# Graph attention: fp32 scores computed once, with targets on partitions, and turned exponentials

## What is computed

```python
q = (x @ wq + bq).reshape(n, H, C)        # H = 2, C = 64; k and v alike
alpha = einsum('ehc,ehc->eh', q[dst], k[src]) / sqrt(C)
amax  = segment_max(alpha, dst)           # 0 where a node has no edge
ex    = exp(alpha - amax[dst])
a     = ex / (segment_sum(ex, dst)[dst] + 1e-16)
out   = segment_sum(a[:, :, None] * v[src], dst).mean(axis=1) + x @ ws + bs
```

## Time and profile before

| | |
|---|---|
| median of the runs | 8686.94 us |
| span of the profiled execution | 8694.1 us |
| mean granted clock of TensorE | 0.789 of full speed |
| busy: TensorE, VectorE, ScalarE, GpSimd | 73%, 64%, 15%, 37% of the span |
| first attention layer: features, start, loop | 3889 to 3949, 3949 to 3983, 3983 to 4827 us |
| second attention layer: features, start and loop | 4842 to 4901, 4901 to 5783 us |

### The profile page before, as it was taken

How to read it: one execution, slowest core, us unless ns; L and a number is a source line. 1 busy time by engine, 2 the same in 40 slices (tenths; PEclk the granted TensorE clock), 3 DMA queues, 4 the chain that set the end, 5 groups by cost and what they waited for, 6 DMA issues and landing times. The chain is left out here.

```text
span 8694.1 us, 138919 instructions
## 1 busy us (share of the span) xinstructions
PE 6376.9 (73%) x36273; PEld 3791.6 (44%) x36274; DVE 5552.2 (64%) x10618; ACT 1317.8 (15%) x3535; POOL 3238.2 (37%) x3402
## 2 busy tenths in 40 slices
PE   7999998734444444449999899986677767667776
PEld 3444446634433443436777567752222223222222
DVE  8888887355555555537777677755555554555556
ACT  0010003100000100012222322221111111111111
POOL 0000000027676776740000000006666664666666
PEclk8999998855555555558999899988878887788877
DMA  0000003522222221111111011111111112111111
GB/s 17 15 18 16 15 15 145 210 73 55 54 51 55 54 55 49 48 32 50 45 45 49 28 53 45 45 50 22 21 21 21 21 21 45 20 22 21 21 21 22
DMA packets 281353, 367.04 MB, mean 42 GB/s; under 512 B 197704, under 2 KB 203578, under 8 KB 281274
## 3 DMA queue, kind: packets, MB, share of 16 engines
q1 hardware_dynamic: 179882, 202.80, 7.3%
q0 software_dynamic: 97792, 142.80, 7.2%
q10 hardware_dynamic: 3600, 20.48, 0.6%
HBM read 309.36 MB, written 56.51 MB: 42 GB/s over the span
## 5 line engine op out<-in xcount | busy, mean ns | idle before, releaser
L1685 POOL DMA_INDIRECT r0s_got<-rel_h,r0s_now x880 | 924.8, 1051 | 2459.4 <-ACT r0s_now L1672 2082.2
L972 POOL DMA_INDIRECT en_got<-edge_q,en_now x1296 | 1294.8, 999 | 413.0 <-issue 368.8
L405 PE MATMUL ps_count<-hot_s,hot_d 128*128 128x512 bf16 (+1 forms) x6160 | 1260.1, 360 | 44.5 <-ACT rows L435 21.8
L1771 PE MATMUL r1s_ps<-r1s_typed,r1s_hot 128*128 128x512 f32 x1760 | 964.8, 700 | 412.1 <-DVE r1s_typed L1722 345.6
L1771 PE MATMUL r0s_ps<-r0s_typed,r0s_hot 128*128 128x512 f32 x1760 | 969.6, 702 | 402.1 <-DVE r0s_typed L1722 331.1
L1685 POOL DMA_INDIRECT r1s_got<-rel_h,r1s_now x880 | 926.2, 1053 | 515.0 <-issue 234.4
L1161 PE MATMUL en_t<-ident,en_got 128*128 128x128 f32 x1296 | 359.3, 433 | 857.5 <-DVE en_got L1055 681.1
L388 DVE TENSOR_SCALAR hot_s<-iota_s,srcm 128x3200 bf16<-128x3200 f16 x880 | 921.4, 1047 | 0.0
L405 PEld LDWEIGHTS ps_count<-hot_s,hot_d 128*128 128x128 bf16 x6160 | 542.1, 98 | 607.4 <-ACT rows L435 72.0
L1771 PEld LDWEIGHTS r1s_ps<-r1s_typed,r1s_hot 128*128 128x128 f32 x1760 | 364.3, 219 | 1011.9 <-DVE r1s_typed L1722 517.8
L1771 PEld LDWEIGHTS r0s_ps<-r0s_typed,r0s_hot 128*128 128x128 f32 x1760 | 364.7, 220 | 1006.3 <-DVE r0s_typed L1722 547.5
(11 more groups left out here) (330 smaller groups left out, 8729.6 us busy)
## 6 DMA issues: line engine op xcount, KB each, us to landing
en_got<-edge_q,en_now POOLq DMA_INDIRECT x1296
count_rows<-rows SPq DMA_DIRECT2D x25, 800.0 KB
c0s_rows<-count_rows SPq DMA_DIRECT2D x25, 800.0 KB, 4.6
count_panels<-c0s_panel ACTq DMA_DIRECT2D x25, 800.0 KB
c1s_rows<-count_rows SPq DMA_DIRECT2D x25, 800.0 KB, 6.1
c1s_panel<-count_panels SPq DMA_DIRECT2D x25, 800.0 KB, 7.6
en_raw<-count_panels SPq DMA_DIRECT2D x25, 800.0 KB
a0s_rows<-count_rows SPq DMA_DIRECT2D x25, 800.0 KB, 5.7
```

Source lines behind the costliest of these rows:

```text
L405: pe.matmul(ps[:, c:c + wd], hot_d[:, j, :], hot_s[:, j, c:c + wd], start=fresh, stop=True, skip_group_check=True)
L972: pool.indirect_dma_start(out=got[:, i, j, :], out_offset=None, in_=k.q[:, :], in_offset=bass.IndirectOffsetOnAxis(ap=now[i][:, j:j + 1], ...
L1685: pool.indirect_dma_start(out=got[:, j, :], out_offset=None, in_=k.h[:, :], in_offset=bass.IndirectOffsetOnAxis(ap=now[:, j:j + 1], axis=0 ...
L1771: pe.matmul(ps[:, ds(w % 2, 1), :].rearrange("p a c -> p (a c)"), hot[:, j, :], typed[j][:, :, :].rearrange("p r d -> p (r d)"), start=fre ...
```

## The change

The three-part split goes. q (already scaled) and k are kept in fp32 with the two heads on partitions 0 to 63 and 64 to 127 (`qt`, `kt`), and v loses its ones. A score is computed once, in fp32, with targets on partitions, one matmul for each head over its 64 partitions. One VectorE instruction masks a slice and takes its maximum (`veil`), into `seen`, which now holds both heads of all 3200 sources in two buffers. ScalarE takes the exponential in place with the maximum as bias (`power`), in four chunks of 5 to 8 blocks. One VectorE instruction weighs a chunk by the count rows and sums it for the denominator (`weigh`). TensorE turns the weighted exponentials, 4 tiles of 128x128 a unit (`turn`), ScalarE copies them out (`line`), and TensorE sums with v as the stationary operand, one head to output partitions 0 to 63, the other to 64 to 127 (`sum_up`); the result is turned back (`turn_back`). Panels are no longer loaded. The count rows have two buffers; they are now used by the mask and by the weighing. The mask and a copy of q's window move to GpSimd. The diff, cut to its core:

```diff
-            def score(w, u, i):
-                for n, (q, key) in enumerate(score_products(k)):
-                    last = pe.matmul(sps[i % 2][:, 0:wd], q[:, h, ds(w * P, P)], key[:, h, c:c + wd],
-                                     start=(n == 0), stop=(n == 2))
+            def score(w, u, i):
+                c, wd = SLICES[i]
+                wait_alone(pe, veiled, w * NS + i + 1, passed_e)
+                for h in range(2):
+                    last = pe.matmul(sps[(u + i) % 2][h][:, 0:wd], qw[u][h * D:(h + 1) * D, :],
+                                     k.kt[h * D:(h + 1) * D, c:c + wd], start=True, stop=True)
-            def shift(w, u, i):
...
+            def turn(w, u, j):
+                wait_alone(pe, lined, w * NU + slot_before(j) + 3, passed_e)
+                wait_alone(pe, weighed, w * NC + chunk_of[j] + 1, passed_e)
+                for i in range(n):
+                    for h in range(2):
+                        last = pe.transpose(tps[slot(j)][:, (2 * i + h) * P:(2 * i + h + 1) * P],
+                                            seen[u][:, h, (b + i) * P:(b + i + 1) * P], k.ident[:, :])
+            def sum_up(w, u, j):
+                wait_alone(pe, lined, w * NU + j + 3, passed_e)
+                for i in range(n):
+                    for h in range(2):
+                        last = pe.matmul(ops[u][h * D:(h + 1) * D, 0:P], k.va[:, b + i, h * D:(h + 1) * D],
+                                         ext[(u + j) % 2][:, (2 * i + h) * P:(2 * i + h + 1) * P],
+                                         start=(j == 0 and i == 0), stop=(j == NU - 1 and i == n - 1))
+            def window(w, u, following):                                  # TensorE
+                scores = [[0, 1], [2, 3], [4, 5], [6]] if following else [[]] * NC
+                for c, (a, b) in enumerate(CHUNK):       # CHUNK = [(0, 3), (3, 7), (7, 10), (10, NU)]
+                    for i in scores[c]:
+                        score(w + 1, 1 - u, i)
+                    for j in range(a, b):
+                        turn(w, u, j)
+                        if j >= 1:
+                            sum_up(w, u, j - 1)
+                    if c == 0 and not (isinstance(w, int) and w == 0):
+                        turn_back(w - 1)
+                sum_up(w, u, NU - 1)
+            def veil(w, u, i):                                            # VectorE
+                if i == 0:
+                    wait_alone(v, masked, w + 1, passed_v)
+                wait_alone(v, scored, w * NS + i + 1, passed_v)
+                for h in range(2):
+                    last = v.tensor_tensor_reduce(seen[u][:, h, c:c + wd], sps[(u + i) % 2][h][:, 0:wd],
+                                                  no_row[u][:, c:c + wd], 1.0, -3.0e38, ALU.add, ALU.max,
+                                                  most[u][:, h, i:i + 1])
+            def weigh(w, u, c):
+                wait_alone(v, expd, w * NC + c + 1, passed_v)
+                for h in range(2):
+                    last = v.tensor_tensor_reduce(seen[u][:, h, a:b], seen[u][:, h, a:b], rows[u][:, a:b], 1.0, 0.0,
+                                                  ALU.mult, ALU.add, den[u][:, h, c:c + 1])
+            def window(w, u, following):
+                slices = [[0, 1], [2, 3], [4, 5], [6]] if following else [[]] * NC
+                for c in range(NC):
+                    for i in slices[c]:
+                        veil(w + 1, 1 - u, i)
+                    weigh(w, u, c)
+                    if c == 0 and not (isinstance(w, int) and w == 0):
+                        finish(w - 1, 1 - u, (w + 1) * TOP + (w - 1) * FINISH)
...
+            with sp.Fori(0, W - 3, 2) as w:                               # SyncE
+                sp.wait_ge(weighed, w * NC + NC)
+                load(w + 2, 0)
+                sp.wait_ge(weighed, w * NC + 2 * NC)
+                load(w + 3, 1)
+            def ready(w, u):                                              # GpSimd
+                pool.tensor_copy(qw[u][:, :], k.qt[:, ds(w * P, P)]).then_inc(q_ok, 1)
+                wait_alone(pool, rows_in[u], (w - u) * 8 + 16, passed_p)
+                pool.tensor_scalar(no_row[u][:, :], rows[u][:, :], 0.0, NEG, ALU.is_equal, ALU.mult).then_inc(masked, 1)
```

More of the change, by code:

```diff
@@ L1252, in _ @@
         def _(pe):
[L1253 to L1261, removed]
+            pe.wait_ge(loaded, 16 * 8)
+            for s, (c, wd) in enumerate(SLICES):
+                for t, kept_ in enumerate((q_kept, k_kept)):
+                    if s >= 2:
+                        pe.wait_ge(kept_, s - 1)
+                    pe.matmul(qk[2 * t + s % 2][:, 0:wd], wqk[:, t, :], k.xt[:, c:c + wd],
+                              start=True, stop=True).then_inc(products, 1)
@@ L1285, in _ @@
[L1285 to L1292, removed]
+            for s, (c, wd) in enumerate(SLICES):
+                act.wait_ge(products, 2 * s + 1)
+                act.activation(k.qt[:, c:c + wd], qk[s % 2][:, 0:wd], ACT.Copy, scale=D ** -0.5).then_inc(q_kept, 1)
@@ L1294, in _ @@
+            for n, (w, m) in enumerate(VS):
+                act.wait_ge(values, n + 1)
+                both = vs[n % 4][:, 0:m * KV].rearrange("p (j c) -> p j c", j=m)
+                act.activation(k.va[:, w:w + m, :], both[:, :, 0:H], ACT.Copy)
+                act.activation(k.z[:, w:w + m, :], both[:, :, H:KV], ACT.Copy).then_inc(kept, 1)
         @block.vector
         def _(v):
[L1296 to L1316, removed]
@@ L1335, in attention @@
         sem = lambda n: k.sem(f"{name}_{n}")
-        rows = sb("rows", [P, NP], BF16)
-        no_row = [sb(f"no_row{u}", [P, NP], BF16) for u in range(2)]
[L1338 to L1344, removed]
+        NS = len(SLICES)
@@ L1464, in _ @@
-            for i in range(NPT):
-                score(0, 0, i)
-            turn_top(0)
-            def window(w, u, following, after):
-                for i in range(NU):
-                    if following:
-                        for part in BESIDE[i]:
-                            score(w + 1, 1 - u, part)
-                    shift(w, u, i)
-                    if i >= 2:
-                        sum_up(w, u, i - 2)
-                    if i == NU - 2 and following:
-                        turn_top(w + 1)
-                sum_up(w, u, NU - 2)
+            pe.sem_inc(lined, 2)
@@ L1543, in finish @@
                 v.sem_inc(done, 1)
-            FINISH = 4
-            v.memset(ones[:, :], 1.0)
-            mask(0, 0)
-            mask(1, 1)
-            for i in range(NPT):
-                veil(0, 0, i)
-                if i >= 1:
-                    part_max(0, i - 1)
-            part_max(0, NPT - 1)
-            find_top(0)
-            def window(w, u, following, after):
-                own.at(TOP + w * (TOP + FINISH))
-                for i in range(NU):
-                    beside = BESIDE[i] if following else []
-                    for part in beside:
-                        veil(w + 1, 1 - u, part)
-                    if following and i == NU - 2:
-                        find_top(w + 1)
-                    weigh(w, u, i)
-                    for part in beside:
-                        part_max(w + 1, part)
-                    if i == 3 and after:
-                        mask(w + 2, u)
-                finish(w, u)
+            FINISH = 5
```

312 lines of the change are left out of this document (146 added, 166 removed).

## The result

The changed kernel takes 9503.1 us (median of 4 runs, 9492 to 9513), the kernel before 8682.2 on the same chip: ratio 1.0932, 95% interval 1.0909 to 1.0956, 821 us more. The profiled execution spans 9490.3 us. From the first turning of the nodes to the one ahead of the relation stage, which takes in both attention convolutions, it went from 1924.3 to 2744.7 us, +820.4. The spans of the two profiled executions differ by 796.2 us (8694.1 before), so all of the loss lies in this part, and the other stages took 24 us less between the two executions.

The account below looks back on a forecast made before the run. TensorE was taken to bound the old loop; after the change engines take turns, so a window sums its waits to 47 us. Two stages of 25 windows, less 43 us of features, give +532 us, 9220; range 8850 to 9650.

Parts of the forecast that it names:

- P: Time of one target window in the attention convolutions' loop, 25 windows each; forecast 47 us, break-even 36.4.
- 50P - 1818: Change in total time from both attention stages and the shorter features; +532 us for P = 47.
- (a): Window start: row load 5.0 us, GpSimd's mask 3.5, handoffs 0.7, then two veils and a weighing 4.7; together 13.9.
- (b) to (d): Chunk-to-chunk steps of turns, sums, scores, veils and weighing: 11.0, 12.0, 6.7 us; overlapped heads 9.6, 9.8, 5.4.
- changes of shape: TensorE switching between matmul shapes within a window: 0.1 us each, some 22 times, 2.2 us.
- half-and-half clock: Loop spends half its time at either clock level: (40.9 + 53)/2 = 47 us a window, heads overlapped.
- The sums: TensorE's sums of weighted exponentials with v: 0.21 us each at full clock, half that if the heads overlap.
- The accumulator's second instruction: VectorE's fetch of the accumulated value after each mask-and-maximum or weighing pass; taken as 0.09 us.
- rival 2: TensorE stays at 1.2 GHz (53 us a window, 9519) or halves do not overlap (67, 10219); chance 0.22.
- Rival 3: TensorE and VectorE work beside one another, scores ready ahead of turns: window 27 to 30 us, 8320; chance 0.07.
- rival 1: Full clock and full overlap of the heads in the loop: 40.9 us a window, +227, 8914; chance 0.18.
- one in-order queue: Argument against TensorE and VectorE working side by side: each engine's queue runs in order, with a weighing in every cycle.

Follow-up runs that it names:

- e1: Changed kernel with the mask made on VectorE, right before a window's first veil, in place of GpSimd; 9198.9 us, ratio 1.0444.
- e6: Changed kernel with each head's scores multiplied over all 128 rows, the other head's queries zero; 9580.3 us, ratio 1.1033.
- e10: e5 with VectorE's and ScalarE's order mended, plus each head's scores multiplied over all 128 rows, the other head's queries zero; 8379.4 us, ratio 0.9544.
- e11: Changed kernel with the mask on VectorE and two slices of scores a chunk earlier, rows still landing late; 8446.2 us, ratio 0.9616.
- e5: Changed kernel with rows loaded early, scores a chunk earlier, division and VectorE's mask for the window after next behind the second weighing; 8145.3 us, ratio 0.9371.
- e3: Changed kernel with only TensorE's order changed: two slices of scores a chunk earlier, ahead of the turns; 9009.1 us, ratio 1.0232.
- e2: Changed kernel with GpSimd making the mask a window ahead, from an extra buffer loaded early; 9558.9 us, ratio 1.0857.
- e4: Changed kernel with GpSimd's mask early, scores a chunk earlier and the division behind the second weighing; 8725.3 us, ratio 0.9914.

## Why the prediction was right, and where it was off

The sign, the mechanism and the range held: 821 us were measured and 533 forecast, P is 52.9 (13 masks from 4504.39 to 5139.01 us) where 47 was said, and 50P - 1818 gives +827 for the measured P. One term was badly mis-sized, the mask in (a), and it is why 533 became 821.

- **(a), GpSimd's mask.** 3.5 us were taken, with 5.6 as the upper bound; it takes 11.0. The nearest GpSimd row, an operation without an input, was no bound for one that reads and writes bf16. The load (4.3 to 4.6 us, 5.0 said) and the handoff were right, so the start wait is 16.2 and not 9.2: 7.0 us of P, 350 us of the time. e1 takes 8.6 us of P away by removing 10 of them.
- **(b) to (d).** Said was 24.8 us with the heads overlapped, 27.0 with the changes of shape, and 33.1 with half of the loop at either clock; 12.0, 11.9 and 8.8 are measured, 32.7 (clock 0.77, 0.80 and 0.68). The start's two veils and weighing are 4.2 (4.7 said). Without the start wait P is 36.7, where 47 - 9.2 = 37.8 was forecast: the half-and-half clock was a fair estimate (0.74 measured).
- **Inside (b) to (d), two errors nearly cancel.** The changes of shape were charged 0.1 us 22 times, 2.2; in the window shown the weight loads stand idle at 17 changes for 4.7 us, some 0.17 each at the upper clock and 0.33 at the lower. VectorE's veils and weighings were charged 12.7 us and take 10.9: the second score of a pair is ready in time, and a veil of both heads takes 1.22 where 1.4 was said.
- **The sums** write halves of the output's partitions, and the overlapped estimate took them at half. That came out: eight records one after another would be 0.86 us at full clock, and a unit of them starts 0.59 before the next operation, 0.17 of it the change, so 0.42. That it is overlap and not another cause is argued from these rows; only for the scores was it tried (e6, e10).
- **The accumulator's second instruction** is 0.08 us, 0.09 said, but it costs next to nothing: passes with it start 0.61 apart, where 0.60 and 0.09 were added. The features take 37.3 us at 0.50 (38 said). The stage's start is 34 us, not 25, with two masks one behind the other; the first and last windows give most of that back.
- **The upper end of rival 2** does not follow from its terms. One after another, TensorE's visible part of (b) to (d) is 4.8, 6.8 and 4.2 us and the changes 2.2, which makes 64 of the 45.8 at 1.2 GHz, not 67. The forecast does not rest on it.
- **The waits** came as listed: four for weighings, three for scores, one for the mask, no engine above 60%. The wait for the mask was put at 7 to 10 us and is 15.8.
- **The rivals.** Rival 3, VectorE and TensorE beside one another, is not what this order does, but what the design can do: e11 reached P 29.2, within its 27 to 30, and e5 24.8, under them. The overlap half of rival 1 was true, its clock not. The "one in-order queue" argument was right for the order as written and would have been wrong as a statement on the edit's idea: the loss is the order's, and moving two slices of scores and GpSimd's one instruction turns +9% to -4% (e11). The formula itself holds along the way: for e3's P of 40.3 it gives +197 us, and 0.0232 of 8684 is 201; for e5's 24.8 it gives -578, and -546 is measured.

What stays open is whether half rows have any part in the clock's fall beside the idle stretches: e5's loop has 64-row scores at 1.00, e6's 128-row ones at 0.81, and in e6 TensorE is also busy for more of the time (58% against 54%).

## What to carry to other kernels

When work goes to fewer, longer instructions, ask of each queue what stands in front of the instruction that the other engine waits for. Here less work on TensorE cost 9%, because scores lay behind turns (7 points, e3) and the mask on a slow engine (5 points, e1). The same work with its scores one chunk earlier, its mask on VectorE, its rows loaded early and its division later gains 6% (e5). And price an operation on an engine that has none in the trace from a row with the same inputs, or leave its upper bound open. A slow instruction on a side engine can cost on the chain (e1) and, if it is moved off the chain, through what it blocks beside it (e2).

## What the runs showed of the hardware

- GpSimd's two-operation pass over 128 x 3200 bf16 takes 10.99 us, with one operation 8.29; VectorE makes it in 0.99.
- A VectorE pass with two operands in SBUF that meets it takes 8.1 to 11.4 us in place of 0.95 (e2, e4) and, in the window shown, ends 0.5 us after it; one with an operand in PSUM keeps its 0.69.
- fp32 matmuls of two heads on halves of the rows overlap: two slices in 1.99 us, over all rows 3.60 to 3.70, both at a granted clock of 1.00 (2.4 GHz).
- The granted clock rises as the waits go: 0.74, 0.93 and 1.00 in the loops of the changed kernel, e11 and e5, which do the same matmuls per window. Two waits removed together gave 2.5 us of P more than each by itself (e11 against e1 and e3).
- VectorE's read of an accumulator is a record of 0.08 us, but passes over 512 columns with it start 0.61 us apart; before, without it, two took 1.28 us, 0.60 apart.
